# First mixture of a four-layer network: DVE's first product stays in PSUM, TensorE runs four units ahead, the last zero writes move between the last batch's reads

## The reference

```python
topk_idx, topk_w = _gate(x, gate_w, gate_bias)        # 8 of 32 experts, from 2 of 4 groups
g = einsum('th,eih->eti', x, expert_gate)             # 32 experts, 64 hidden columns each
u = einsum('th,eih->eti', x, expert_up)
outs = einsum('eti,ehi->eth', silu(g) * u, expert_down)
final = (take_along_axis(outs, topk_idx) * topk_w).sum(1)
shared = (silu(x @ shared_gate.T) * (x @ shared_up.T)) @ shared_down.T
x = x + tanh(g_ffn[0]) * (final + shared)             # x on the right is normalised
```

## Time and profile before

| | |
|---|---|
| median of 3 runs | 866.94 us (864.4 to 868.1) |
| profiled execution, its span | 865.67 us, 863.9 us |
| PE, DVE, ACT, POOL busy | 746.3, 572.4, 375.6, 397.9 us of the span |
| the first mixture | about 117 to 295 us |
| granted clock of PE, mean | 0.943 of full speed |

### The profile page before, as it was taken

How to read it: one execution, slowest core, us unless ns; L and a number is a source line. 1 busy time by engine, 2 the same in 40 slices (tenths; PEclk the granted TensorE clock), 3 DMA queues, 4 the chain that set the end, 5 groups by cost and what they waited for, 6 DMA issues and landing times.

```text
span 863.9 us, 13706 instructions
## 1 busy us (share of the span) xinstructions
PE 746.3 (86%) x3871; PEld 535.3 (62%) x3872; DVE 572.4 (66%) x1797; ACT 375.6 (43%) x834; POOL 397.9 (46%) x381
## 2 busy tenths in 40 slices
PE   7989888998988768977999787999989989898995
PEld 3567666776766536654888786565645544555663
DVE  3377879898899378862633575978776644344564
ACT  0244343545454345625445334547455655313441
POOL 2000034546457534363774343656346764244772
PEclk9899999999999889966999998999999999799998
DMA  5011659394946931014577751000330000013325
GB/s 147 13 50 53 218 172 289 100 312 136 286 155 180 312 94 31 20 59 144 164 212 217 204 148 57 3 1 1 86 97 14 13 13 14 13 39 78 102 69 146
DMA packets 84826, 96.38 MB, mean 112 GB/s; under 512 B 19881, under 2 KB 63536, under 8 KB 84626
## 3 DMA queue, kind: packets, MB, share of 16 engines
q1 hardware_dynamic: 78544, 86.54, 34.8%
q0 software_dynamic: 5024, 8.54, 2.9%
q10 hardware_dynamic: 1186, 0.43, 0.2%
HBM read 57.25 MB, written 40.12 MB: 113 GB/s over the span
## 4 chain that ended last, share of the span: by engine, by line
PE 48%; DVE 29%; issue 8%; POOL 5%; ACT 4%; DMA 4%; SPq 1%; ACTq 0%; DVEq 0%; POOLq 0%
PE psum L1228 43%; DVE hb L2389 3%; DVE hb L2382 3%; POOL s L767 2%; PE psum L1685 2%; POOL s L789 1%; DVE hb L2380 1%; DVE xn L1935 1%; POOL h_lo L726 1%; DVE mr L2033 1%; DVE const L1989 1%; DVE stats L1922 1%; DMA y<-xn 1%; DMA l_hi<-in_pack 1%; DVE l_lo L1949 1%
## 5 line engine op out<-in xcount | busy, mean ns | idle before, releaser
L726 POOL TENSOR_TENSOR h_lo<-hb,h_hi 128x512 fp32r<-128x512 f32 x68 | 95.6, 1418 | 77.8 <-ACT h_hi L962 77.4
L1228 PE MATMUL psum<-xt_hi,wa_hi 128*128 128x512 f32 x272 | 126.1, 464 | 4.6 <-DVE hb L2380 4.2
L794 POOL DMA_INDIRECT y<-xn x93 | 92.2, 991 | 65.3 <-DVE xn L2125 34.2
L1228 PE MATMUL psum<-xt_lo,wa_hi 128*128 128x512 f32 x272 | 108.2, 398 | 0.0
L721 POOL TENSOR_TENSOR hb<-hb,wsb 128x512 f32<-128x512 f32 x64 | 82.1, 1284 | 55.1 <-DVE hb L2380 48.2
L944 ACT ACTIVATE hb<-psum 128x512 f32<-128x512 f32 x136 | 80.4, 591 | 54.0 <-PE psum L1228 53.4
L698 POOL TENSOR_TENSOR rstd<-veps,neghalf 128x4 f32<-128x4 f32 x20 | 20.3, 1016 | 124.1 <-DVE veps L1927 123.7
L962 ACT ACTIVATE h_hi<-hb 128x512 fp32r<-128x512 f32 x68 | 42.9, 630 | 70.2 <-DVE hb L2389 67.4
L2380 DVE TENSOR_TENSOR hb<-hb,psum 128x512 f32<-128x512 f32 x68 | 46.0, 684 | 38.8 <-ACT hb L944 27.9
L1228 PE MATMUL psum<-hb,wa_hi 128*128 128x512 f32 x136 | 70.0, 595 | 0.5 <-POOLq L723 0.5
L2389 DVE TENSOR_TENSOR hb<-hb,l_lo 128x512 f32<-128x512 f32 x64 | 67.5, 1055 | 3.2 <-DMA l_lo<-wd 1.1
(11 more groups left out here) (356 smaller groups left out, 1688.5 us busy)
## 6 DMA issues: line engine op xcount, KB each, us to landing
s<-l_lo SPq DMA_DIRECT2D x20, 1386.0 KB, 9.4
l_lo<-wd SPq DMA_DIRECT2D x128, 128.0 KB, 3.1
l_hi<-in_pack SPq DMA_DIRECT2D x24, 322.0 KB, 3.3
l_lo<-in_pack SPq DMA_DIRECT2D x22, 322.0 KB, 3.4
xn<-s SPq DMA_DIRECT2D x93, 66.0 KB, 2.0
stage<-in_pack SPq DMA_DIRECT2D x13, 256.0 KB, 2.6
y_in<-y SPq DMA_DIRECT2D x8, 256.0 KB, 3.7
l_hi<-y SPq DMA_DIRECT2D x8, 256.0 KB, 5.1
```

The lines of the kernel that those rows point to most:

```text
L726: pool.tensor_tensor(h_lo[:, k % 3, :], hb[:, k % 4, :], h_hi[:, k % 3, :].bitcast(F32), ALU.subtract).then_inc(q["hlo_pool"], 1)
L794: pool.indirect_dma_start(y3, bass.IndirectOffsetOnAxis(xe3[:, j % XE, 128:129].bitcast(I32), 0), xe3[:, j % XE, 0:128], None, bounds_chec ...
L1228: return pe.matmul(o, l, r, start=start, stop=stop, skip_group_check=True)
```

## The change

In units 1 to 16 DVE's first product overwrites the up product in its PSUM bank, and the second reads it from there and writes hb. The up bank is free for PE only when the whole unit is done, so `gu` waits for `h_done` in place of `um_done`; unit 0 has one product as before, straight to hb. `um_done` now counts the units of layer 2 only, and its users there are renumbered. PE issues four units ahead in layer 0 and three, as before, in layer 2. Steps of layer 0 on ACT and DVE move by one unit; on PE, comb_in moves from unit 13 to 12. The zero writes after units 8, 10, 12 and 14 are issued in batch 3 too; one of the last five is left, and stands right behind the last batch's reads.

```diff
-        ROUTE_AT = {0: (5, 6, 7, 9, 10, 11, 11, 12, 12), 2: (8, 8, 8, 8, 8, 9, 10, 11, 12)}
-        WEIGH_AT = {0: 13, 2: 14}
+        ROUTE_AT = {0: (6, 7, 8, 10, 11, 12, 12, 13, 13), 2: (8, 8, 8, 8, 8, 9, 10, 11, 12)}
+        WEIGH_AT = {0: 14, 2: 14}
...
-        AHEAD = 3
+        AHEAD = {0: 4, 2: 3}
...
-                        if b + 1 < B and c in Z_AFTER:
+                        if c in Z_AFTER:
                             zero_rows(Z_FIRST + b * len(Z_AFTER) + Z_AFTER.index(c))
+                for i in range(Z_FIRST + B * len(Z_AFTER), NZ):
+                    zero_rows(i)
...
-                    for i in range(Z_FIRST + (B - 1) * len(Z_AFTER), NZ):
-                        zero_rows(i)
...
                     if k >= 3:
-                        pe.wait_ge(q["um_done"], k - 2)
+                        pe.wait_ge(q["h_done"], k - 2)
                     product(U0[k % 3][:, :], us).then_inc(q["u_done"], 1)
...
-                dve.tensor_tensor(h, h, U0[k % 3][:, :], ALU.mult).then_inc(q["um_done"], 1)
-                dve.wait_ge(q["um_done"], k + 1)
+                u = U0[k % 3][:, :]
                 if c == 0:
-                    dve.sem_inc(q["h_done"], 1)
+                    dve.tensor_tensor(h, h, u, ALU.mult).then_inc(q["h_done"], 1)
                     return
                 w = b * ROUTED[0] + c - 1
+                link(dve.tensor_tensor(u, h, u, ALU.mult))
                 dve.wait_ge(d_wb[w % WS], 32 * (w // WS + 1))
-                dve.tensor_tensor(h, h, wrow[:, w % WS, :], ALU.mult).then_inc(q["h_done"], 1)
+                dve.tensor_tensor(h, u, wrow[:, w % WS, :], ALU.mult).then_inc(q["h_done"], 1)
```

More of the change, by code:

```diff
@@ L497, in knum @@
             return CB[l] + b * NC[l] + c
-        NORM_AT, OUT_AT, XN_AT, TAIL_XT_AT, PE_TAIL_XT = 0, 2, 3, 5, 2
-        XHI_AT, XLO_AT, SCORE_AT = {0: 3, 2: 5}, {0: 3, 2: 6}, {0: 4, 2: 8}
-        ROUTE_AT = {0: (5, 6, 7, 9, 10, 11, 11, 12, 12), 2: (8, 8, 8, 8, 8, 9, 10, 11, 12)}
-        WEIGH_AT = {0: 13, 2: 14}
+        NORM_AT, OUT_AT, XN_AT, TAIL_XT_AT, PE_TAIL_XT = 0, {0: 3, 2: 2}, 3, 6, 2
+        XHI_AT, XLO_AT, SCORE_AT = {0: 4, 2: 5}, {0: 4, 2: 6}, {0: 5, 2: 8}
+        ROUTE_AT = {0: (6, 7, 8, 10, 11, 12, 12, 13, 13), 2: (8, 8, 8, 8, 8, 9, 10, 11, 12)}
+        WEIGH_AT = {0: 14, 2: 14}
         COMBT_AT = {0: 15, 2: 16}
-        PE_XN, PE_LOGITS, PE_RUN, PE_COMB = {0: 0, 2: 2}, {0: 1, 2: 5}, 11, {0: 13, 2: 13}
+        PE_XN, PE_LOGITS, PE_RUN, PE_COMB = {0: 0, 2: 2}, {0: 1, 2: 5}, 11, {0: 12, 2: 13}
         def pe_back(l, b):
@@ L510, in add_at @@
         def add_at(l, b):
-            return 8 if l == 0 and b < B - 1 else 3
+            if l == 0:
+                return 9 if b < B - 1 else 4
+            return 3
         NORM2_AT, XN2_AT = 4, 7
-        AHEAD = 3
+        AHEAD = {0: 4, 2: 3}
         def fft_steps(l, b):
@@ L712, in low @@
                 if l == 2:
-                    pool.wait_ge(q["um_done"], k + 1)
+                    pool.wait_ge(q["um_done"], k - CB[2] + 1)
                     if c >= ROUTED[2]:
@@ L1192, in _ @@
                             unit(l, b, c)
-                            if c == OUT_AT and b >= 1:
+                            if c == OUT_AT[l] and b >= 1:
                                 out_t(l, b - 1)
@@ L1495, in gu @@
                 if k - CB[2] >= 2:
-                    pe.wait_ge(q["um_done"], k - 1)
+                    pe.wait_ge(q["um_done"], k - CB[2] - 1)
                 else:
@@ L1875, in _ @@
                         pe.wait_ge(q["shared2"], 1)
-                    for c in range(AHEAD):
+                    for c in range(AHEAD[l]):
                         gu(l, 0, c)
@@ L1879, in _ @@
                         for c in range(NC[l]):
-                            k = b * NC[l] + c + AHEAD
+                            k = b * NC[l] + c + AHEAD[l]
                             if k < B * NC[l]:
```

## The result

The changed kernel takes 860.72 us (median of 20 runs, 854.9 to 866.8) against 866.74 of the kernel before (20 runs): ratio 0.9942, 95% interval 0.9915 to 0.9969. It is faster, by 6.0 us instead of the forecast 15. The profiled execution's span is 859.0 us, 4.9 less than before.

What follows compares the result with a forecast made beforehand. It took a ring of waits between POOL, ACT, DVE and PE, closed by POOL stopping DVE's second product, as the bound; 13.9 us from three stretches plus 1.3 from the last batch made 15.2, so about 852 us, range 849 to 856.

Steps and rivals of the forecast that it cites:

- Products: DVE's two products in 64 units of the first mixture: each priced at 0.69 us, the second no longer stopped by POOL.
- PE after the transpose: PE's work from comb_in to the next batch's unit 6 up product: 16.1 us, with DVE holding nobody.
- DVE's run to wfin: DVE from unit 6 to the end of wfin in each batch: 24.1 us, with routing's waits for POOL left unchanged.
- routing is held up more: Rival: POOL holds small routing instructions in units 6 to 14, wfin 1.3 to 3.9 us later; 856 to 864; chance 0.16.
- PE's stall at comb_in: PE, with 21.5 us of work before the weights' transpose, would stand there 2.6 us a batch waiting for wfin.
- Zero writes: Four writes between the last batch's reads: unit 16 waits 3.2 us for its row; removing them from 277 us gains nothing.
- The sum: Whole mixture: 4.6 us less in each of three stretches, together 13.9, plus 1.3 in the last batch: 15.2 us.
- reads more than 42 us apart: Sign of being wrong: the batches' weight reads, forecast 40 us apart, starting more than 42 us apart.

Runs made afterwards that it cites:

- short_low: Changed kernel with POOL's low part covering 8 of 512 columns in units 5 to 13 of the first three batches; ratio 0.9851 to the kernel before.
- product_only: Kernel before with only the first product left in PSUM; three units ahead, steps and zero writes as before; ratio 0.9836 to the kernel before.
- ahead_only: Kernel before with the product in PSUM and PE four units ahead, routing steps and zero writes unmoved; ratio 0.9814 to the kernel before.
- Pe_filler: Changed kernel, last batch's zero writes moved back, nine throwaway matmuls in front of the transpose of the weights; ratio 0.9815 to the kernel before.
- zeros_in_again: Changed kernel, its zero writes kept between the last batch's reads, wfin in front of unit 14's products; ratio 0.9881 to the kernel before.
- weigh_early: Changed kernel, last batch's zero writes moved back, wfin in front of unit 14's products; ratio 0.9811 to the kernel before.
- zeros_back: Changed kernel with the last batch's zero writes moved back behind the second stage load; ratio 0.9855 to the kernel before.
- shift_only: Changed kernel's order (four ahead, shifted steps) with both products in SBUF and zero writes as before; ratio 0.9990 to the kernel before.
- spread: Kernel before with product in PSUM, PE four ahead, routing one step behind each unit to unit 14, wfin and transpose one unit later; ratio 0.9890.
- no_eps: Changed kernel, last batch's zero writes moved back, wfin before unit 14, the 1e-20 addition left out of the first mixture's routing; ratio 0.9791.

## Why the prediction was right and wrong

*Products: right.* The second is 0.691, forecast 0.69, the first 0.695, forecast 0.69. The price that the Trainium skill would have put on PSUM (Perfetto Trace Analysis, Optimizing Scalar/DVE Operations: some 65 ns of access more than SBUF) isn't there: against L2389 of before at its shortest, 691, the first product takes 4 ns more at its median.

*PE after the transpose: right.* What PE has to do there was put at 16.1 us together; from 156.85 to the end of unit 6's up product at 173.2 it took 16.4.

*DVE's run to wfin: the step that failed.* The prediction said "Routing instructions that wait for POOL [...] I leave as they are", and had wfin done 24.1 us after unit 6's up product. It was done at 198.87, 25.6 after 173.2. The 1.5 us are the longer holds (4.8 against 3.3). In short_low, where POOL's instructions in these units are cut to 0.2 us, all holds and the stall are gone. This is the rival "routing is held up more", to which the prediction gave 0.16 and 1.3 to 3.9 us. Its reason against that rival, that the steps keep their order behind each product, doesn't bear: they keep it in product_only (3.8 us lost), in ahead_only (4.0) and in the changed kernel (4.8). What counts is whether POOL is in its 1.3 us when a step is issued, and that moves with everything. Nor are two SBUF operands, of which the rival speaks, all that is held: L2221, one of its two examples, is a TENSOR_SCALAR that reads one. In the three batches the holds take 1.0, 1.5 and 1.7 us more than before, 4.2 of the missing 8.1.

*PE's stall at comb_in: right in size by luck, and its price left out.* Forecast 2.6, measured 2.46 to 2.72. With wfin 1.5 later it would have been 4, but in batch 1 PE came to the transpose 23.2 us after unit 6's up product, not 21.5: it had stood 0.62 and 0.24 for DVE's second products, and lost the other 0.9 in matmuls a little further apart than 0.227. Two errors of about one size hide in the stall. What the step left out is the clock behind it: 1.6 us in batch 2 of this profile. Pe_filler speaks for the stall as the cause. The clock of the runs is lower too: 0.933 over 20 runs of the changed kernel, 0.941 and 0.942 over the runs of the kernel before and of product_only; within the 20 runs a span goes up by 4.4 us for 0.01 less (fit, correlation -0.92). How much of that comes from the transposes isn't shown: short_low has no stall there and 0.932.

*Zero writes: mechanism right, size short.* The wait comes as forecast, 2.6 at unit 16 where 3.2 was forecast, but unit 14 waits 3.7 ahead of it. The queue issues 18 reads, the rows of nine units, ahead of the first of the four zero writes, so the third and the fourth stand just ahead of the rows of units 14 and 16. The last product ended 39.4 us after the reads began, not 38.0; without the zero writes it is 35.6, or 34.3 where the clock stays up, near the 34.8 that the forecast implied (38.0 - 3.2). The change thus pays 3.8 to 5.0 for them and not 3.2 (zeros_in_again against weigh_early, where the clock stays up in the last batch of both, gives the 5.0), and that the forecast called taking four writes off 277 us worth nothing was right: the later stages didn't get shorter. Why the last product had to start 38.7 us after the reads began, and not 37.3, stays open: in batch 1 of the changed kernel the transfers ended 37 us after they began (the DMA engines' share is 0.65 from 196 to 197 us, then 0.07). In the last batch the engines are still full when unit 16's row comes (1.06 from 283 to 284 us), and the fifth zero write and two stage loads are issued right behind that row; that these take its bandwidth was not tried.

*The sum.* Short of the forecast by stretch: 4.6 - 3.4 = 1.2, 4.6 - 2.85 = 1.75, 4.6 - 0.8 = 3.8, 1.3 + 0.1 = 1.4; together 8.1. The holds explain 1.0, 1.5 and 1.7 of the first three, the clock 1.6 of the third, the zero writes the last; 0.3 in each of the three is what PE took longer behind the transpose, if batch 1 speaks for all. The direction, the flat products, the stall's place and the wait in the last batch were right, and reads more than 42 us apart were among the signs named for being wrong.

*What the forecast did not ask* is which part of the change earns the time. Three ahead with the steps where they were, PE has no stall over 1.14 us in the mixture, keeps its clock there, and the product alone gives 0.9836.

## What to carry to other kernels

Where one engine's instruction stops another's, taking one victim away doesn't take all of the stop away: here the products run free, and routing loses 4.8 us a batch instead of 3.3. Count which instructions will stand at that moment afterwards, and price the stop per POOL instruction, not per line. A planned stall of TensorE has to be priced with the clock behind it, and a change of several parts with each part alone: here one part took 14 us off the mixture, and the other two gave back 7 (the order 1.6, with two falls of the clock in its profile, and the zero writes 5.4).

## What was not expected of the hardware

TensorE's clock fell from 2.4 to 1.2 GHz for 2.7 to 4.9 us behind six of nine stalls of 2.2 to 3.2 us at the transposes (changed kernel 1 of 3, zeros_back 2 of 3, shift_only 3 of 3). Behind shorter stalls in the same stretch of the batches it fell once (1.9 us, shift_only) and else not; three of 1.8 to 2.1 us in spread are among these. Apart from these it falls, up to the mixture's last product, only once, at about 127 us in seven of the thirteen traces, the one of before included, behind the logits of batch 0, where PE has stood 0.3 to 0.5 us (2.0 in shift_only); zeros_back and no_eps have the same 0.46 us there and no fall. So a stall can be followed by the low clock, and needn't be.

Which DVE instructions POOL's subtraction stops: in these traces TENSOR_TENSOR with both operands in SBUF and TENSOR_SCALAR with one (0.17 to 1.25 us for 128x4), but never RECIPROCAL (0.18 in the routing), MAX8 or MATCH_REPLACE8, which ran wholly within one of POOL's subtractions 6, 12 and 69 times, nor a TENSOR_TENSOR with one operand in PSUM (0.67 to 0.70 for 128x512). TENSOR_REDUCE kept its 0.27 to 0.29 too, but met POOL in only 3 of 39 cases, and those in part. The Trainium skill (SBUF — State Buffer, Who interferes with whom) says that a DVE instruction with two SBUF inputs contends with a GpSimd instruction that reads SBUF, that tensor_scalar can contend, and that tensor_reduce never does on this chip. The trace agrees on the first two, and on the third as far as those 3 cases go.
